# Windowed attention on one core: a 64-row score per head, probabilities turned by VectorE in blocks of 32, and a mix in four row groups

## What is computed

```python
q, k, v = split(x @ Wqkv)                    # 16 heads of 64
q = l2norm(q) * q_scale;  k = l2norm(k) * k_scale
q, k = rotary(q), rotary(k)
# windows of 32 tokens; a query sees its own window and the one before
sim  = einsum('bhwie,bhwje->bhwij', bq, bk2) * 8     # 32 queries x 64 keys
sim  = where(mask, -max, sim)
attn = softmax(sim, -1)
out  = einsum('bhwij,bhwje->bhwie', attn, bv2)
x    = x_shifted + out @ Wo
```

## Time and profile before

| | |
|---|---|
| time, median of 3 runs | 4558.43 us (4558.27 to 4563.87) |
| profiled execution | 4560.67 us |
| its span, first to last instruction | 4558.9 us |
| mean granted TensorE clock | 0.956 |
| PE busy, share of the span | 4228.4 us, 93% |
| DVE busy | 3608.9 us, 79% |
| ACT busy | 3009.7 us, 66% |
| POOL busy | 2849.6 us, 63% |

### The profile page before, as it was taken

One profiled execution on the slowest core, in us unless ns is written; L12 is line 12 of the kernel. 1 busy time (PEld: TensorE's weight loads), 2 busy tenths in 40 slices (PEclk: granted clock), 3 DMA queues, 4 the chain that ended last, 5 costly groups with the idle time before them and its releaser, 6 DMA issues.

```text
span 4558.9 us, 86667 instructions
## 1 busy us (share of the span) xinstructions
PE 4228.4 (93%) x32672; PEld 2902.5 (64%) x32672; DVE 3608.9 (79%) x4102; ACT 3009.7 (66%) x4797; POOL 2849.6 (63%) x1551
## 2 busy tenths in 40 slices
PE   5888889888759999999999999999999999999998
PEld 2333333333347777777877777777777777777775
DVE  3888898889867888787887888788887888878784
ACT  5655555555347777777777777777777777777774
POOL 0555455555457677676776767766676666766662
PEclk8898898988869999999999999999999999999999
DMA  1000000000010110001100010000100011000001
GB/s 37 0 0 0 0 0 0 0 0 0 19 44 22 33 31 22 22 22 33 31 22 25 19 43 22 23 23 20 45 19 25 22 33 30 19 25 22 22 22 49
DMA packets 144208, 96.47 MB, mean 21 GB/s; under 512 B 11694, under 2 KB 136624, under 8 KB 142776
## 3 DMA queue, kind: packets, MB, share of 16 engines
q1 hardware_dynamic: 143800, 90.93, 6.5%
HBM read 74.02 MB, written 16.88 MB: 20 GB/s over the span
## 4 chain that ended last, share of the span: by engine, by line
PE 68%; issue 2%; ACT 1%; POOL 1%; DVE 1%; DMA 0%; SPq 0%; ACTq 0%; POOLq 0%; DVEq 0%
PE ps L860 15%; PE ps L780 12%; PE ps L846 9%; PE ps L791 8%; PE ps L818 8%; PE ps L885 5%; PE ps L828 4%; PE ps L898 3%; PE ps L807 2%; PE ps L867 1%; PE ps L873 1%; PE ps L799 1%; PE ps L763 0%; ACT sq L950 0%; ACT w_qk L920 0%
## 5 line engine op out<-in xcount | busy, mean ns | idle before, releaser
L1269 POOL TENSOR_TENSOR resid<-resid,rnorm 128x1024 f32<-128x1024 f32 x384 | 726.8, 1903 | 537.4 <-DVE rnorm L1094 537.4
L425 POOL TENSOR_TENSOR read<-state,c_row 128x1024 f32<-128x1024 f32 x256 | 598.4, 2356 | 619.6 <-DVE state L411 494.7
L1259 POOL TENSOR_TENSOR resid<-resid,sq 128x1024 f32<-128x1024 f32 x384 | 909.0, 2372 | 101.8 <-DVE resid L1122 101.8
L860 PE MATMUL ps<-mixed,w_vo 128*128 128x128 f32 x6144 | 722.5, 276 | 4.2 <-ACT hidden L1042 2.7
L860 PEld LDWEIGHTS ps<-mixed,w_vo 128*128 128x128 f32 x6144 | 701.0, 192 | 21.6 <-issue 21.6
L780 PE MATMUL ps<-w_qk,xs_parts 128*128 128x512 f32 x2304 | 638.5, 413 | 38.9 <-DVE resid L1122 13.3
L229 PE MATMUL mamba_ps<-read,ident 128*128 128x512 f32 x1024 | 569.5, 695 | 22.4 <-DVE xc L366 19.8
L1122 DVE TENSOR_TENSOR resid<-ps,rope_l 128x1024 f32<-128x1024 f32 x384 | 467.5, 1217 | 112.9 <-ACT sq L950 109.9
L950 ACT ACTIVATE sq<-ps 128x1024 f32<-128x1024 f32 x384 | 394.3, 1027 | 239.6 <-PE ps L780 232.9
L1109 DVE TENSOR_TENSOR sq<-ps,rope_l 128x1024 f32<-128x1024 f32 x384 | 467.2, 1217 | 78.5 <-ACT sq L950 75.9
L780 PEld LDWEIGHTS ps<-w_qk,xs_parts 128*128 128x128 f32 x2304 | 417.8, 192 | 156.8 <-issue 68.2
(11 more groups left out here) (140 smaller groups left out, 6908.9 us busy)
## 6 DMA issues: line engine op xcount, KB each, us to landing
x_rows<-row_scratch SPq DMA_DIRECT2D x384, 128.0 KB, 2.8
row_scratch<-rows SPq DMA_DIRECT2D x192, 64.0 KB, 2.2
w_stage<-w_qk_hbm SPq DMA_DIRECT2D x6, 1024.0 KB, 5.9
vo_stage<-w_v_hbm SPq DMA_DIRECT2D x6, 512.0 KB, 4.0
vo_stage<-w_o_hbm SPq DMA_DIRECT2D x6, 512.0 KB, 4.8
xn<-x_hbm SPq DMA_DIRECT2D x4, 512.0 KB, 5.4
kept<-resid SPq DMA_DIRECT2D x8, 256.0 KB, 3.1
resid<-kept SPq DMA_DIRECT2D x8, 256.0 KB, 4.3
```

Source lines behind the costliest of these rows:

```text
L425: pool.tensor_tensor(read[:, u % 4, :], state[:, u % 4, :], c_row[:, (u // 2) % 2, :], ALU.mult).then_inc(read_ready, 1)
L860: last = pe.matmul(bank[:, 0:P], w_vo[:, 2 * a + h, :], mixed[:, odd, a, h, :], start=a + h == 0, stop=a == PAIRS - 1 and h == 1)
L1259: pool.tensor_tensor(qk[:, tile % 2, cols], qk[:, tile % 2, cols], sq[:, 2 + part, :], ALU.add).then_inc(done[f"rotated{part}"], 1)
L1269: pool.tensor_tensor(heads, heads, norms, ALU.mult).then_inc(done[f"normed{part}"], 1)
```

## The change

- **Score.** Each head has its own matmul on its own 64 rows: 16 heads times 4 windows, 64 weight rows by 32 columns, 64 moving columns. Heads on rows 0 to 63 write one bank, those on rows 64 to 127 the other. `k_t` loses its zero halves and its two copies; it keeps three tiles in place of two.
- **Turning the probabilities.** `prob_turn0/1` on PE and `copy_probs0/1` on ACT go. One VectorE instruction a tile, `turn_probs`, transposes the 128x1024 probabilities in blocks of 32x32.
- **Mix.** One stage in place of two: for each window its own 32 rows of keys and the 32 rows of the window before, so 8 matmuls of 32 rows, 128 weight columns and 512 moving columns, the four windows on four row groups into four banks, accumulated over the two. `copy_mixed0..3` are four copies of 512 columns, one a window.
- **Rows.** `row_turn` does two transposes (x, and x one window back), `copy_rows` one copy of both. The DMAs to and from DRAM go, and with them the `x_rows` tile and six stores at the start.
- **Banks.** The two banks of the mix join the rotation: four banks in rotation; a mix or a fold takes all four, each use waits for the reader of the one four uses before.
- The four orders are written anew.

The diff, cut to its core:

```diff
-K_RING = 2
+K_RING = 3
+def head_at(place):
+    return place % PAIRS * 2 + place // PAIRS
 PE_ORDER = [
+    (1, 0, "row_turn"), (0, 0, "project0"), (2, 3, "mix"), (1, 2, "score"), (0, 0, "project1"), (2, 2, "output"),
...
+    (0, 0, "head_turn0"), (3, None, "ff_output"), (0, 0, "head_turn1"), (1, 0, "output"), (0, 0, "head_turn3"),
+    (1, 2, "row_turn"), (0, 0, "head_turn2"), (0, 2, "project1"), (1, 1, "mix"), (0, 0, "score"), (0, 3, "project0"),
+    (1, 2, "mix"), (0, 1, "head_turn1"), (0, 1, "head_turn0"), (0, 1, "head_turn3"), (0, 1, "head_turn2"),
...
 ACT_ORDER = [
...
+    (2, 1, "copy_mixed2"), (2, 1, "copy_mixed1"), (2, 1, "copy_mixed3"), (2, 1, "copy_mixed0"), (2, 3, "exponent"),
+    (1, 3, "square0"), (2, 2, "copy_mixed0"), (2, 2, "copy_mixed1"), (2, 2, "copy_mixed2"), (2, 2, "copy_mixed3"),
+    (1, 1, "copy_heads1"), (1, 1, "copy_heads0"), (1, 1, "copy_heads3"), (1, 1, "copy_heads2"), (1, 2, "inverse_norm"),
...
+TURN_BANKS = 4
 def turn_banks(pe):
-    turns = [x for x in pe if x[0] in TURN_READERS]
-    return {x: (k % 2, (TURN_READERS[turns[k - 2][0]], turns[k - 2][1]) if k >= 2 else None) for k, x in enumerate(turns)}
+    uses = [(name, k, i) for name, k in pe if name in TURN_READERS or name in ("mix", "fold")
+            for i in range(TURN_BANKS if name in ("mix", "fold") else 1)]
+    return {x: (n % TURN_BANKS, uses[n - TURN_BANKS] if n >= TURN_BANKS else None) for n, x in enumerate(uses)}
...
-                sp.dma_start(row_scratch[l, WINDOW + t * P:WINDOW + (t + 1) * P, :], rows[:, odd, :]).then_inc(rows_stored, 16)
-                for h in range(2):
-                    sp.dma_start(x_rows[64 * h:64 * h + 64, odd, :, :], seen).then_inc(rows_loaded, 16)
...
-                pe.transpose(bank[:, 0:P], shifted(xa, t * P, P), ident[:, :]).then_inc(done["row_turn"], 1)
+                first = column(t * P)
+                for back in (WINDOW, 0):
+                    to = bank[:, 0:P] if back else bank[:, P:2 * P]
+                    last = pe.transpose(to, xa[:, first - back:first - back + P], ident[:, :])
+                last.then_inc(done["row_turn"], 1)
...
                 for a in range(PAIRS):
                     for w in range(WINDOWS):
-                        last = pe.matmul(to, q_t[:, odd, a, w * WINDOW:(w + 1) * WINDOW], keys, start=False, stop=True,
-                                         skip_group_check=True)
+                        for h in range(2):
+                            rows_h = slice(64 * h, 64 * h + 64)
...
+                            last = pe.matmul(ps[w * WINDOW:(w + 1) * WINDOW, S + h, first:(a + 1) * 2 * WINDOW],
+                                             q_t[rows_h, odd, a, w * WINDOW:(w + 1) * WINDOW], keys, start=False, stop=True,
+                                             skip_group_check=True)
...
+            def mix(tile):
+                after(pe, ("turn_probs", tile), ("copy_rows", tile))
+                banks = [turn_free("mix", tile, w) for w in range(WINDOWS)]
+                for own in range(2):
+                    for w in range(WINDOWS):
+                        rows_w = slice(w * WINDOW, (w + 1) * WINDOW)
+                        last = pe.matmul(banks[w], rows[rows_w, tile % 2, own, :], prob_t[rows_w, tile % 2, :, own, :],
+                                         start=own == 0, stop=own == 1)
+                last.then_inc(done["mix"], 1)
...
-                    act.copy(k_t[0:64, tile % K_RING, pairs, 0, :], bank[0:64])
-                    act.copy(k_t[64:128, tile % K_RING, pairs, 1, :], bank[64:128]).then_inc(done[name], 1)
+                    dst = q_t[:, tile % 2, pairs, :] if c < 2 else k_t[:, tile % K_RING, pairs, :]
+                    act.copy(dst, bank).then_inc(done[name], 1)
...
+            def copy_mixed(w):
+                def stage(tile):
+                    after(act, ("mix", tile))
+                    if tile >= 2:
+                        after(act, ("output", tile - 2))
+                    act.copy(mixed[:, tile % 2, :, w * WINDOW:(w + 1) * WINDOW], turn_bank("mix", tile, w).rearrange(
+                        "p (h n) -> p h n", h=HEADS)).then_inc(done[f"copy_mixed{w}"], 1)
+                return stage
...
+            def turn_probs(tile):
+                after(dve, ("normalise_probs", tile))
+                if tile >= 2:
+                    after(dve, ("mix", tile - 2))
+                dve.transpose(prob_t[:, tile % 2].rearrange("p h o n -> p (h o n)"),
+                              prob[:, tile % 2].rearrange("p h k -> p (h k)")).then_inc(done["turn_probs"], 1)
...
-            pool.memset(k_t[:, :], 0.0).then_inc(const_set, 1)
```

More of the change, by code:

```diff
@@ L818, in score @@
-                        last = pe.matmul(to, q_t[:, odd, a, w * WINDOW:(w + 1) * WINDOW], keys, start=False, stop=True,
-                                         skip_group_check=True)
-                last.then_inc(done["score"], 1)
-            def prob_turn(c):
-                def stage(tile):
-                    after(pe, ("normalise_probs", tile))
-                    bank = turn_free(f"prob_turn{c}", tile)
-                    for j in range(4):
-                        a = 4 * c + j
-                        last = pe.transpose(bank[:, j * P:(j + 1) * P],
-                                            prob[:, tile % 2, 2 * a:2 * a + 2, :].rearrange("p h k -> p (h k)"), ident[:, :])
-                    last.then_inc(done[f"prob_turn{c}"], 1)
-                return stage
@@ L833, in mix @@
-            def mix(r):
-                def stage(tile):
-                    if r:
-                        after(pe, ("copy_mixed0", tile))
-                    else:
-                        after(pe, ("copy_probs0", tile), ("copy_probs1", tile))
-                        pe.wait_ge(rows_loaded, 32 * tile + 32)
-                        if tile:
-                            after(pe, ("copy_mixed1", tile - 1))
-                    pe.wait_ge(vo_copied, 4 * sum(("fold", l) in PE_SEQ[:PE_SEQ.index((f"mix{r}", tile))] for l in range(DEPTH)))
-                    for w in (2 * r, 2 * r + 1):
@@ L844, in stage @@
                         for h in range(2):
                             rows_h = slice(64 * h, 64 * h + 64)
-                            last = pe.matmul(ps[:, G + h, (w % 2) * 256:(w % 2 + 1) * 256],
-                                             x_rows[rows_h, tile % 2, w, :], prob_t[rows_h, :, w * WINDOW:(w + 1) * WINDOW],
-                                             start=True, stop=True, skip_group_check=True)
-                    last.then_inc(done[f"mix{r}"], 1)
-                return stage
+                            own = k_t[rows_h, tile % K_RING, a, w * WINDOW:(w + 1) * WINDOW]
@@ L852, in output @@
             def output(tile):
                 l, t, odd = place(tile)
-                after(pe, ("copy_mixed0", tile), ("copy_mixed1", tile))
+                after(pe, *[(f"copy_mixed{w}", tile) for w in range(WINDOWS)])
                 if t == 0:
@@ L857, in output @@
                 bank = turn_free("output", tile)
-                for a in range(PAIRS):
-                    for h in range(2):
-                        last = pe.matmul(bank[:, 0:P], w_vo[:, 2 * a + h, :], mixed[:, odd, a, h, :],
-                                         start=a + h == 0, stop=a == PAIRS - 1 and h == 1)
+                for place_h in range(HEADS):
+                    last = pe.matmul(bank[:, 0:P], w_vo[:, head_at(place_h), :], mixed[:, odd, place_h, :],
+                                     start=place_h == 0, stop=place_h == HEADS - 1)
                 last.then_inc(done["output"], 1)
@@ L901, in _ @@
             stages = {"fold": fold, **indexed("project", project, 2), **indexed("head_turn", head_turn, 4),
[L902 removed]
+                      "row_turn": row_turn, "score": score, "mix": mix,
                       "output": output, "mean": mean, "variance": variance,
@@ L981, in copy_rows @@
                 if tile >= 2:
-                    act.wait_ge(rows_stored, 16 * (DEPTH + tile - 1))
-                else:
-                    act.wait_ge(rows_stored, 16 * DEPTH)
-                act.copy(rows[:, tile % 2, :], turn_bank("row_turn", tile)[:, 0:P]).then_inc(done["copy_rows"], 1)
+                    after(act, ("mix", tile - 2))
+                act.copy(rows[:, tile % 2, :, :], turn_bank("row_turn", tile)[:, 0:2 * P].rearrange(
+                    "p (b n) -> p b n", b=2)).then_inc(done["copy_rows"], 1)
             def exponent(tile):
```

158 lines of the change are left out of this document (65 added, 93 removed), and 37 rows, old and new, of tables (ACT_ORDER, DVE_ORDER, PE_ORDER, POOL_ORDER).

## The result

The changed kernel takes 4587.96 us (median of 5 runs, 4582.95 to 4588.57) against 4562.26 (5 runs, 4558.27 to 4563.87) of the kernel before: ratio 1.0055, 95% interval 1.004 to 1.007. It is slower by 0.55%, a little but more than the runs scatter, where 4326 us was forecast. The profiled execution took 4588.57 us.

The account below looks back on a forecast made before the run. PE was taken to bound 192 equal tiles: 16.67 us less changes gave 15.07, plus 0.21 bank waits and 0.17 disturbance, 15.45; over 191 steps 233 us less, 4327.7, so 4326 us by median. Range 4215 to 4480.

Parts of the forecast that it names:

- 13.39 + 1.21 = 14.60 us: DVE per tile: 13.39 us busy in the old kernel plus 1.21 for the new transposition of the probabilities.
- for DVE and PE disturbing each other I add 0.17: Allowance of 0.17 us a tile in the time sum for delays between nearly level DVE and PE.
- 16.67 - 15.45 over 191 steps: Whole gain: old less new tile time, times 191 steps, 233 us, taken off the profiled 4560.67 us.
- the score (1.42 for 1.30): PE's score stage, 128 small load and matmul pairs: 1.30 us a tile where it was 1.89, saving 0.59.
- the mix (1.93 for 1.96): PE's mix stage, 16 passes on four row groups side by side: 1.96 us a tile, 0.16 less than before.
- The bank waits: PE's head turns after tile 2's mix wait for ACT's copies of shared banks: 0.84 us a chunk, 0.21 a tile.
- Rival B: Score at its low end, 1.03 us, most bank waits hidden: 14.90 us a tile, 4220 us; chance 0.20.
- Rival D: Score's small pairs paced by issue, 2.99 us at 22 ns each: slower, 4616 us, or 4767 at 29.5 ns; chance 0.11.
- Rival E: Mix's four row groups run two at a time, 3.75 us: 17.07 us a tile, 4635 us; chance 0.04.
- Rival C: DVE becomes the bound, transposition at 2.37 us or DVE not filled beyond 90%: 16.16 us a tile, 4461 us; chance 0.15.
- nearly level, so either one's delay can now reach the other: PE at 15.07 and DVE at 14.60 us a tile follow written orders, so delays can pass between them.
- Fold and output ... taken as nothing: Fold and output on PE: same matmuls, fold's second half no longer waits for copies, 1.2 us a layer, under 7 in all.

Follow-up runs that it names:

- The reductions in the same places: Changed kernel with the three Newton operations as reductions over an axis of length one, Newton step left out: 4356.96 us, ratio 0.9542 to the kernel before.
- the transposition twice: Changed kernel with `refine`, fold and POOL order moved, plus a second 128 by 896 VectorE transposition per tile into an unread buffer: 4452.03 us, against 4351.57 without it.
- the collisions of `refine` and the boundary mended: Changed kernel with `refine` of tile 1 earlier, the boundary fold later and POOL's `normed` of tile 0 first: 4351.57 us, ratio 0.9539 to the kernel before.
- the low part earlier: Changed kernel with `refine`, fold and POOL order moved, plus POOL's low part of w_qk before the last tile's rotated: 4343.55 us, ratio 0.9516.

## Why the prediction was wrong

**The step that failed** is "13.39 + 1.21 = 14.60 us" for DVE, and with it the range. The 1.21 was right (1.236). The 13.39 was taken from the old order and assumed to hold in the new one. It does not: three operations that nobody edited cost 1.6 us a tile more, because how long they last depends on what POOL does at that moment, and the change rewrote the orders. The 13.39 also held a cost of the same kind, 0.3 us at the guard (L1082, 531 ns; L1048, 216 ns), which the new order happened to take away. 13.39 + 1.24 + 1.60 - 0.31 is 15.92; durations that overlap by 0.2 us more bring it to the 15.68 measured, in place of 14.60. In the sum for the time the term for this is "for DVE and PE disturbing each other I add 0.17": PE's waits for L1088 alone are 90.3 / 118 = 0.77 us a tile, and PE's lower clock comes on top. The steps are 16.74.

**The account.** The profiled execution came out 4588.57 - 4327.7 = 261 us over the sum. The steps took 16.74 for 15.45, 247 us. The reductions in the same places took 231 us off, so that much of it is the holding and what it sets off (PE's waits, its lower clock). Another 17 us is an error of the sum itself: it took 16.67 - 15.45 over 191 steps, where 16.67 was the mean of the stretch shown and the whole had 16.58. The part outside the steps gave 3 back (1394.3 before, 1391.1 after).

**Point by point.**
- PE's stages: the score (1.42 for 1.30) and the mix (1.93 for 1.96) were right, and L828 is gone. The bank waits were right in place and size: 0.8 us, once a chunk.
- Rival B needed a score of 1.03 us; it came out at 1.42.
- Rival D (small pairs paced by their issue, 2.99 us) is refuted: 128 pairs in 1.42 us are 11 ns each. The sign came out as D's, by another mechanism. Rival E is refuted by the mix's step.
- Rival C had the right engine and the wrong reason: it priced the transposition at up to 2.37 us. That DVE's 15.68 is near its 15.76 is chance. Its limit of filling DVE to 90% does not hold either (96% with the transposition twice).
- Near the right question and not asked there: the earlier trace rows and the sentence "nearly level, so either one's delay can now reach the other". The trace before did show the mechanism in one place, the guard of the norm (L1082, 531 ns in the mean beside 226 for its neighbours of the same size): 58 of its 192 runs took over 0.5 us, and each ended 0.05 us after a POOL operation. PE was busy for 99% of that stretch all the same, so I take it to have cost nothing then; I did not read it.
- "Fold and output ... taken as nothing" was wrong at the boundary: the fold's fourth bank waited for `add_output`. Moving it gained 31 us in one kernel and 24 in the other.
- With the collisions of `refine` and the boundary mended, the average step is 15.48 us (2956.7 / 191), against 15.45 forecast, and 15.46 with the low part earlier. So close a match is partly luck: the steady chunk is 60.9 / 4 = 15.22, and the boundaries add the rest.

**What the Trainium skill says to it.** The page "SBUF — State Buffer", section Who interferes with whom, calls the port pair that VectorE and GpSimd share an exclusive lock: the one that issues first has it for its whole instruction and the other is blocked; a VectorE instruction with two inputs in SBUF contends with a GpSimd instruction that reads SBUF, `tensor_scalar` can contend, `tensor_reduce` on this chip never does. The traces agree on each form: 2.29 us beside 0.19 for two sources, 1325 ns in the mean for one source and a constant, 187 for the reduction. They show the holding, not the port. That page was not weighed in the prediction, and by it the question "which of DVE's operations will run beside POOL's in the new order" could have been put. Here the holding lasts to the end of POOL's running operation, up to 2.4 us. The page "TensorEngine Tiling (Array Packing)", section Instruction Overhead, gives each matmul some 60 cycles; taken pair after pair that is an estimate of 3.2 us for the score. Across eight groups of the array it does not hold so: 1.42 us.

## What to carry to other kernels

Where one engine can hold another up, as GpSimd does VectorE here, the busy time of one from the old trace carries over only if their operations meet as before: look in the old trace for operations of one form and size with a mean well above their shortest, find what ran beside them, and follow where the new order puts each. Where a hand-written order places small operations of VectorE right behind the one that releases GpSimd, move them ahead of it, or let GpSimd's next operation be the one that waits for them; an engine's busy time does not tell its work from such holding. And take the mean per step and the number of steps from the same stretch.

## What the runs showed of the hardware that was not expected

- Small VectorE operations from SBUF to SBUF (two sources, or one source and a constant, 128x32) last until GpSimd's running operation ends: up to 2.4 us in place of 0.19 (97 of 192 runs of L1058, and none of the 95 that began with GpSimd idle). Reductions of the same size (0.19 us), large VectorE operations that read PSUM (1.21 to 1.23 us) and the transposition in blocks (1.23 to 1.25) are the same beside a running GpSimd operation. It works the other way too: L1249 took 2.05 us the 47 times that a VectorE operation of 0.46 us (L1144) was running as it began, and 1.89 to 1.95 the other 145.
- Pairs of weight load and matmul on eight parts of the array (64 rows by 32 columns) follow each other every 11 ns (1.42 us / 128). Four row groups of 32 with 512 columns each run side by side with no loss that shows (1.93 us for 16, where four in a row are 4 x 0.447).
- A wait of 3.1 us on TensorE was followed in 25 of 44 cases by a slower next stage: in the one looked at, 3.4 us at a granted clock of 0.53, and 1.25 us more for the stage. An idle stretch that looks harmless beside a fuller engine can thus cost more than its length.
